# Three of the products of a fused four-layer graph kernel in float32 from one copy of their input, instead of hi and lo parts in three rounded passes

## The reference

```
L0: qkv = h @ w_qkv, 8 heads of 32; attn = softmax(where(adj == 0, -inf, q k^T * scale))
    o = (attn @ v) @ w_proj + b_proj;   x += o + layernorm(o) * gamma + beta
L1: rel = adj^T * (h Wq^T)(h Wk^T)^T, each row divided by its norm;   x += rel @ (h Wv^T)
L2: hw = h @ W (the GAT weight); e = leaky_relu(hw.a1 + (hw.a2)^T) * adj;
    x += elu(softmax(e) @ hw + beta * hw)
L3: y = adj @ h;   x += y @ weight + bias (the last weight)
```

## Time and profile before

| | |
|---|---|
| median of 3 runs | 1971.55 us (1969.12 to 1973.96) |
| profiled execution, first to last instruction | 1971.0 us (the profile gives its span; the median of the runs lies 0.5 us above it) |
| mean granted TensorE clock | 0.977 of full |
| PE busy | 1831.1 us (93%), 13064 records |
| weight loads busy | 1602.2 us (81%) |
| DVE busy | 1609.3 us (82%), 4485 |
| ACT busy | 1084.3 us (55%), 2756 |
| POOL busy | 674.6 us (34%), 1045 |
| chain that ended last | PE 48%, DVE 25%, issue 15%, POOL 9%, ACT 3% |
| ACT copy with rounding (L559, L599, L652) | 597 to 599 ns each, once a step each (L559 three times) |
| DVE lo part (L699, L778, L854) | 688, 679, 681 ns |

### The profile page before, as it was taken

How to read it: one execution, slowest core, us unless ns; L and a number is a source line. 1 busy time by engine, 2 the same in 40 slices (tenths; PEclk the granted TensorE clock), 3 DMA queues, 4 the chain that set the end, 5 groups by cost and what they waited for, 6 DMA issues and landing times.

```text
span 1971.0 us, 39957 instructions
## 1 busy us (share of the span) xinstructions
PE 1831.1 (93%) x13064; PEld 1602.2 (81%) x13064; DVE 1609.3 (82%) x4485; ACT 1084.3 (55%) x2756; POOL 674.6 (34%) x1045
## 2 busy tenths in 40 slices
PE   6899999999999999999999999999999999999974
PEld 5788888878878888888878878788888878878864
DVE  3688897888888887887888888888887988978874
ACT  3555565655655555655655655655655655655632
POOL 3233333333333333333333333333332333333331
PEclk8999999999999999999999999999999999999987
DMA  2000000000000000000000000000000000000000
GB/s 88 12 17 17 23 23 11 21 16 16 21 17 16 22 16 17 21 16 16 22 16 16 21 17 16 22 16 16 22 16 16 22 16 16 21 16 17 12 6 17
DMA packets 37975, 37.85 MB, mean 19 GB/s; under 512 B 2416, under 2 KB 37488, under 8 KB 37872
## 3 DMA queue, kind: packets, MB, share of 16 engines
q1 hardware_dynamic: 37872, 36.84, 5.7%
HBM read 20.05 MB, written 16.78 MB: 19 GB/s over the span
## 4 chain that ended last, share of the span: by engine, by line
PE 48%; DVE 25%; issue 15%; POOL 9%; ACT 3%; DVEq 0%; POOLq 0%; DMA 0%; ACTq 0%
PE bank L314 15%; PE mid L387 11%; DVE stats L683 6%; DVE x L764 5%; PE bank L322 4%; POOL o_res L909 4%; POOL rstd L899 4%; PE bank L507 3%; PE mid L370 3%; PE bank L512 3%; PE bank L487 3%; DVE x L849 3%; DVE h_t_lo L699 2%; DVE o_gam L756 2%; ACT h_t_hi L559 2%
## 5 line engine op out<-in xcount | busy, mean ns | idle before, releaser
L567 ACT ACTIVATE probs<-mid,neg_max 128x128 f32<-128x128 f32 x1024 | 284.8, 379 | 105.2 <-DVE neg_max L713 105.2
L379 PE MATMUL mid<-k_diag,q_t 128*128 128x512 f32 x512 | 273.6, 617 | 0.0
L559 ACT ACTIVATE h_t_hi<-bank 128x512 fp32r<-128x512 f32 x192 | 114.9, 599 | 251.7 <-PE bank L322 251.6
L387 PEld LDWEIGHTS mid<-v,probs_t 128*128 128x128 f32 x2048 | 244.3, 192 | 3.3
L387 PE MATMUL mid<-v,probs_t 128*128 128x33 f32 x2048 | 239.9, 272 | 0.0
L899 POOL TENSOR_TENSOR rstd<-var_eps,minus_half 128x2 f32<-128x2 f32 x320 | 226.4, 707 | 25.1
L693 DVE TENSOR_SCALAR z<-x,mean_var,rstd 128x256 f32<-128x256 f32 x384 | 205.2, 575 | 10.8 <-POOL rstd L899 3.2
L713 DVE TENSOR_REDUCE neg_max<-mid 128x8 f32<-128x1024 f32 x128 | 154.6, 1208 | 51.1 <-issue 38.0
L897 POOL TENSOR_TENSOR var_eps<-mean_var,eps 128x2 f32<-128x2 f32 x320 | 66.0, 206 | 363.9 <-DVE mean_var L687 363.9
L322 PEld LDWEIGHTS bank<-ident,z 128*128 128x128 f32 x768 | 94.8, 152 | 112.4 <-DVE z L693 73.1
L322 PE MATMUL bank<-ident,z 128*128 128x128 f32 x768 | 125.8, 288 | 61.3 <-DVE z L693 61.3
(11 more groups left out here) (133 smaller groups left out, 5485.0 us busy)
## 6 DMA issues: line engine op xcount, KB each, us to landing
x<-in_x SPq DMA_DIRECT2D x64, 256.0 KB, 2.6
out_x<-x SPq DMA_DIRECT2D x64, 256.0 KB, 2.2
w_qkv_sb<-in_w_qkv SPq DMA_DIRECT2D x1, 768.0 KB, 4.8
w_q_sb<-in_w_q SPq DMA_DIRECT2D x1, 256.0 KB, 5.0
w_k_sb<-in_w_k SPq DMA_DIRECT2D x1, 256.0 KB, 5.3
w_proj_sb<-in_w_proj SPq DMA_DIRECT2D x1, 256.0 KB, 5.2
w_v_sb<-in_w_v_t SPq DMA_DIRECT2D x1, 256.0 KB, 5.4
w_gat_sb<-in_w_gat SPq DMA_DIRECT2D x1, 256.0 KB, 5.7
```

The costliest lines, as they stand in the source:

```text
L379: last = pe.matmul(mid[:, s], q_t[:, par, hc, b * N:(b + 1) * N], k_diag[:, hc, :, b * N:(b + 1) * N], start=False, stop=True)
L387: last = pe.matmul(mid[:, b, h * W33:(h + 1) * W33], probs_t[:, b * HC + h // RG, h % RG], v0[:, par, b, h], start=True, stop=True)
L559: act.activation(h_t[k][0][:], bank[:], ACT.Relu).then_inc(h_hi_ready[k], 1)
L567: last = act.activation(probs[:, s, r], mid[:, s, r * N:(r + 1) * N], ACT.Exp, bias=neg_max[:, s, r:r + 1])
```

## The change

The lo parts of `o_t`, `h_t[2]` and `y_t` and the hi and lo parts of their weights go. ACT copies each input once, in full float32, and PE multiplies it with the float32 weight as it was loaded: `rows_f32`, four float32 matmuls (two graphs, two blocks) for each place, with the input as the stationary, as before. On DVE three operations a step go (L767, L778, L854), on POOL six of the eight operations of `split_weights`. PE waits for the one copy of ACT in place of hi and lo. The ACT copy of `o_t` gets a wait for `o_psum`, which the DVE operation had. Everything else keeps its place.

```diff
@@ -77,10 +77,7 @@
...
         w_qkv_p = parts("w_qkv", [128, C, 3 * D])
-        w_proj_p = parts("w_proj", [128, C, D])
         w_v_p = parts("w_v", [128, C, D])
-        w_gat_p = parts("w_gat", [128, C, D])
-        w_out_p = parts("w_out", [128, C, D])
         w_qk_p = parts("w_qk", [128, C, D])
@@ -115,7 +112,8 @@
...
         z = [sb(f"z{k}", [128, 2, D]) for k in range(3)]
-        h_t = [parts(f"h_t{k}", [128, C, 2 * N]) for k in range(3)]
+        h_t = [parts(f"h_t{k}", [128, C, 2 * N]) for k in range(2)]
+        h_t2_full = sb("h_t2_full", [128, C, 2 * N])
         h_t1_full = sb("h_t1_full", [128, C, 2 * N])
@@ -128,7 +126,7 @@
...
         o_heads = sb("o_heads", [128, 2, D])
-        o_t = parts("o_t", [128, 2, C, N])
+        o_t = sb("o_t", [128, 2, C, N])
         o = sb("o", [128, 2, D])
@@ -156,7 +154,7 @@
...
         h3 = sb("h3", [128, 2, D])
-        y_t = parts("y_t", [128, C, 2 * N])
+        y_t = sb("y_t", [128, C, 2 * N])
         mid = ctx.enter_context(nc.psum_tensor("mid", [128, BC, 512], f32))
...
@@ -200,9 +199,8 @@
...
             sem("u_psum"), sem("u_exp_ready"), sem("x2_exp_ready"), sem("x3_ready"), sem("x3b_ready"))
-        shift3_ready, h3_ready, y_t_psum, y_hi_ready, y_lo_ready, y_psum, x4_ready = (
-            sem("shift3_ready"), sem("h3_ready"), sem("y_t_psum"), sem("y_hi_ready"), sem("y_lo_ready"),
-            sem("y_psum"), sem("x4_ready"))
+        shift3_ready, h3_ready, y_t_psum, y_t_ready, y_psum, x4_ready = (
+            sem("shift3_ready"), sem("h3_ready"), sem("y_t_psum"), sem("y_t_ready"), sem("y_psum"), sem("x4_ready"))
         block = ctx.enter_context(nc.Block())
@@ -258,7 +256,7 @@
...
         ALL_CONSTS = 16 * len(CONSTS)
-        SPLIT = [(w_proj_sb, w_proj_p), (w_v_sb, w_v_p), (w_gat_sb, w_gat_p), (w_out_sb, w_out_p)]
+        SPLIT = [(w_v_sb, w_v_p)]
         def keys_apart(eng, p, half):
@@ -315,6 +313,14 @@
...
                 return last
+            def rows_f32(dst, lhs_t, w, signal):
+
+                for b in range(2):
+                    for c in range(C):
+                        last = pe.matmul(dst[:, b * D:(b + 1) * D], lhs_t(b, c), w[:, c], start=c == 0,
+                                         stop=c == C - 1)
+                last.then_inc(signal, 1)
+
             def transposes(dst, src, k):
@@ -405,17 +411,13 @@
...
                 if relation:
-                    pe.wait_ge(o_hi_ready, done(p3))
-                    pe.wait_ge(o_lo_ready, done(p3))
-                    for b in range(2):
-                        last = product(mid[:, 3, b * D:(b + 1) * D], o_t, w_proj_p,
-                                       lambda a, c: a[:, b, c], lambda a, c: a[:, c])
-                    last.then_inc(o_psum, 1)
+                    pe.wait_ge(o_t_ready, done(p3))
+                    rows_f32(mid[:, 3], lambda b, c: o_t[:, b, c], w_proj_sb, o_psum)
                 if front:
...
                 if middle:
-                    wait_before(pe, o_lo_ready, p2)
+                    wait_before(pe, o_t_ready, p2)
                     wait_before(pe, o_ready, p2)
@@ -442,9 +444,8 @@
...
                 if gat:
-                    pe.wait_ge(h_hi_ready[2], done(p4))
-                    pe.wait_ge(h_lo_ready[2], done(p4))
-                    rows(bank4, h_t[2], w_gat_p, 0, hw_psum)
+                    pe.wait_ge(h2_full_ready, done(p4))
+                    rows_f32(bank4, lambda b, c: h_t2_full[:, c, b * N:(b + 1) * N], w_gat_sb, hw_psum)
                 if front:
@@ -453,9 +454,8 @@
...
                 if last_layer:
-                    pe.wait_ge(y_hi_ready, done(p5))
-                    pe.wait_ge(y_lo_ready, done(p5))
-                    rows(bank7, y_t, w_out_p, 0, y_psum)
+                    pe.wait_ge(y_t_ready, done(p5))
+                    rows_f32(bank7, lambda b, c: y_t[:, c, b * N:(b + 1) * N], w_out_sb, y_psum)
                 if middle:
@@ -588,7 +588,9 @@
...
                 if gat:
-                    relu_hi(2, p4, bank4, [hw_psum])
+                    act.wait_ge(h_t_psum[2], done(p4))
+                    wait_before(act, hw_psum, p4)
+                    act.activation(h_t2_full[:], bank4[:], ACT.Relu).then_inc(h2_full_ready, 1)
                 if front:
@@ -596,7 +598,7 @@
...
                     wait_before(act, y_psum, p5)
-                    act.activation(y_t[0][:], bank7[:], ACT.Copy).then_inc(y_hi_ready, 1)
+                    act.activation(y_t[:], bank7[:], ACT.Copy).then_inc(y_t_ready, 1)
                 if middle:
@@ -649,7 +651,8 @@
...
                     act.wait_ge(o_t_psum, done(p2))
-                    act.activation(o_t[0][:], mid[:, 2], ACT.Copy).then_inc(o_hi_ready, 1)
+                    wait_before(act, o_psum, p2)
+                    act.activation(o_t[:], mid[:, 2], ACT.Copy).then_inc(o_t_ready, 1)
             run(act, step, {1: copy_fold})
@@ -763,8 +766,6 @@
...
                                                  ALU.mult, ALU.add).then_inc(x1_ready, 1)
-                if gat:
-                    relu_lo(2, p4, bank4)
                 if relation:
@@ -773,11 +774,6 @@
...
                     normalize(1, p3, z[1], x1[:, 1 - par], z_ready[1])
-                if last_layer:
-                    dve.wait_ge(y_hi_ready, done(p5))
-                    dve.tensor_tensor(y_t[1][:].rearrange("p c n -> p (c n)"), bank7[:],
-                                      y_t[0][:].rearrange("p c n -> p (c n)").bitcast(f32), ALU.subtract)\
-                       .then_inc(y_lo_ready, 1)
                 if gat:
@@ -848,12 +844,6 @@
...
                                                  x1[:, 1 - par, b], ALU.mult, ALU.add).then_inc(x2_ready, 1)
-                if middle:
-                    dve.wait_ge(o_hi_ready, done(p2))
-                    wait_before(dve, o_psum, p2)
-                    dve.tensor_tensor(o_t[1][:].rearrange("p b c n -> p (b c n)"), mid[:, 2],
-                                      o_t[0][:].rearrange("p b c n -> p (b c n)").bitcast(f32), ALU.subtract)\
-                       .then_inc(o_lo_ready, 1)
                 if gat:
```

More of the change, by code:

```diff
@@ L180, in gnn_stack @@
         h_t_psum = [sem(f"h_t_psum{k}") for k in range(3)]
-        h_hi_ready = [sem(f"h_hi_ready{k}") for k in range(3)]
-        h_lo_ready = [sem(f"h_lo_ready{k}") for k in range(3)]
+        h_hi_ready = [sem(f"h_hi_ready{k}") for k in range(2)]
+        h_lo_ready = [sem(f"h_lo_ready{k}") for k in range(2)]
+        h2_full_ready = sem("h2_full_ready")
         xb_ready, h1_full_ready = sem("xb_ready"), sem("h1_full_ready")
@@ L188, in gnn_stack @@
         heads_psum, inv_sum_ready, o_heads_ready = sem("heads_psum"), sem("inv_sum_ready"), sem("o_heads_ready")
-        o_t_psum, o_hi_ready, o_lo_ready = sem("o_t_psum"), sem("o_hi_ready"), sem("o_lo_ready")
+        o_t_psum, o_t_ready = sem("o_t_psum"), sem("o_t_ready")
         o_psum, o_ready = sem("o_psum"), sem("o_ready")
```

## The result

The changed kernel takes 1955.85 us in the median of seven runs (1949.02 to 1968.49), the kernel before 1971.79 us in seven runs (1969.12 to 1973.96). The ratio is 0.9918, with a 95% interval of 0.9896 to 0.9941: 0.8% faster, 16 us. The forecast was 1952.5 us, range 1944 to 1968. The sign, the size and the range hold. The parts of the sum don't.

The account below looks back on a forecast made before the run. Bound: the dependence loop from w_proj's product through `o`, `x1` and `z[1]` back to PE. 46 x -0.14 and 13 x -0.91 give -18.2, the ends -1: -19 from 1971.55, so 1952.5 us, range 1944 to 1968.

Parts of the forecast that it names:

- Float32's price: At each of three places on PE, eight float32 records take 1.72 us against 1.43 for the rounded passes.
- d: Extra PE time of one place in float32 over three rounded passes: about 0.30 us, bounds 0.29 and 0.45.
- the full-price rival: Float32 places on PE cost a fourth pass, d = 0.45 to 0.48: no change, 1967 to 1971 us; 16%.
- the one with bare loads: Rival: each float32 matmul of a place loses 0.08 us to stationary loads, d = 0.62: slower, 1986 us; 8%.
- w_proj in the ordinary step: PE's longer product with w_proj decides when `o` starts in an ordinary step: 0.17 us later.
- w_gat: Between `x1` and its moments, removing DVE's low part gains 0.61 us; PE's extra 0.30 hides in its wait for `z[1]`.
- `y_t_lo` costed at nothing: After `z[1]` on DVE, removing `y_t_lo` gains nothing, as DVE soon waits for ScalarE; the last weight adds 0.30 us.
- -0.14: Sum for one ordinary step in us: 0.17 - 0.61 + 0.30, counted 46 times.
- The turn: Step after a loop turn: -0.60 for `o_t_lo`, -0.61 and +0.30 give -0.91 us, 13 times.
- the turn swallows its part: Rival: DVE's 2.89 us stall ends at an unmoved time, so a turn brings only -0.31 us: 1960 us; 14%.
- More gain: POOL and DVE get out of each other's way: Rival: POOL and DVE obstruct each other less in `x1` and `z[1]` as their phase moves: about 1940 us; 2%.
- Fill and drain: First and last steps, outside the full steps: together -1 us, between -4 and +3.

Follow-up runs that it names:

- e1: The kernel before with only the w_proj place in float32, w_gat and the last weight left in rounded passes; 1941.99 us, ratio 0.9848.
- e7: The kernel before with only the w_proj place in float32, plus 12 idle instructions before DVE's loop; 1970.28 us, one run.
- e10: The changed kernel with 48 idle instructions on PE alone before the loop; 1953.91 us, ratio 0.9906.
- e9: The changed kernel with 8 idle instructions on DVE and 48 on PE before the loop; 1917.19 us, ratio 0.9723.
- e3_out_only: The kernel before with only the last weight's place in float32; 1980.88 us, ratio 1.0043.
- e12_before_pad245: The kernel before with 245 idle instructions on DVE behind step 2, before the loop; 1996.78 us, ratio 1.0120.
- e8: The kernel before with w_gat and the last weight in float32, w_proj left in three rounded passes; 1903.47 us, ratio 0.9654.
- e5: The changed kernel with 8 idle instructions on DVE before the loop; 1940.7 us, ratio 0.9854.

## Why the prediction was right, and where it was wrong

- **Float32's price.** Right. 1.72 us a place, d = 0.29 to 0.31; the full-price rival and the one with bare loads are out. The page "FP8 and Floating Point Precision" of the Trainium skill, section "TensorE Precision Notes", counts four passes; at the present price of a pass that would be 1.91 us (an estimate). The measurement decides for 1.72.
- **w_proj in the ordinary step.** Right: `o` +0.18 us (forecast +0.17), shown alone by e1 and e7 as +0.19 a step.
- **w_gat.** PE's 0.30 us was hidden in its wait for `z[1]`, as forecast. The removed low part was mis-sized: not -0.61 but -0.49. The moments must now wait until `x1` has landed: `x1` (two instructions) starts at 929.43 and the moments at 931.24, 1.81 later. Before, the low part started 1.69 after `x1` and covered that (DVE of before; the earlier trace rows has the low part at 940.88):

```profile
939.19 1.77 DVE L764 SCALAR_TENSOR_TENSOR x<-o_gam,rstd,o_res 128x256 f32<-128x256 f32 x2
```

- **`y_t_lo` costed at nothing.** This step failed. PE waited for it, 0.21 us in the ordinary step shown. The prediction saw this time, the 0.70 in place of 0.44 behind the transposes of `z[1]`, and read it as the price of a wait; with `y_t_lo` gone it is 0.49. So the last weight costs +0.02 a step and not +0.30. By parts, +0.02 at w_proj, +0.12 at w_gat and -0.28 here turn -0.14 into -0.28; the whole change has -0.255: 5 us more gain.
- **The turn.** This is the term that failed: -0.91 us forecast, -0.24 measured, 13 times: 9 us less gain. At full clock on both sides it is even +0.06; the rest is the slow clock in 8 turns before, which the prediction did not look at. The first part of the step was right; DVE's stall moved with DVE and `o` came 0.55 earlier. But I took the rest of the chain as shifted rigidly. The loop's code had moved, a second stall came with it, DVE's shift fell behind POOL's `o_res`, and the moments of `o` came 1.25 us later than they would have. The rival "the turn swallows its part" gave 1960 us by another mechanism; its number for the turn, -0.31, was nearer than the forecast's. Its reason is refuted: the 2.9 us moved with DVE's arrival, and `o` came earlier.
- **"More gain: POOL and DVE get out of each other's way"** was named with 2%. That their phase can get worse by 1.25 us a turn was not.
- **Fill and drain:** -4.3 against -1, just beyond the bound of -4. Not taken apart.

So the time is right by luck in part: errors of +5, -9 and +3 us nearly cancel. And the 16 us say little of the change's worth: with the same work, the changed kernel ran at 1953.9, 1940.7 and 1917.2 us, depending on idle instructions ahead of its loop. In long turns on both sides the change is worth about 18 us (1972 to 1954), or 21 to 22 without the 3 to 4 us that e10's idle instructions cost. Some 12 of them are the ordinary steps and 7 the slow clock that its turns no longer have; the shift's loss of 1.25 us a turn is already taken off. A comparison in short turns on both sides was not reached. Of the 55 us between before and e9, 0.255 x 59 = 15 come from the steps' work; most of the rest is the turn: 32.29 us before, 29.01 in e9.

What stays open: why the clock falls in some turns of the kernel before and not in others; a test of the condition on the loop's place that is given at the end; why PE's stalls come in some turns only; and the 3 us of fill and drain.

## What to carry to other kernels

Price each place of a change by itself, and look at each of them in the timeline: here one part of three brought all the gain in the ordinary steps, one cost 0.19 us a step, and the best kernel leaves that part out. A wait on several semaphores hides its second operand; an "issue" of 0.24 us on a weight load was a DVE operation that I took as free. In a kernel with a loop, look at the stall at each turn first, in every version that is compared: its length can change with any edit on that engine. The profile's instruction packets and 8 or 12 idle instructions tell whether a difference is the work or the place of the loop. Where steps that do the same work differ in length, look at the granted clock in each before anything else.

## What the runs showed of the hardware

- A turn back costs DVE 0.35 or about 3 us, by where the loop lies in its instruction stream: 0.35 at 449-827, 450-820 and 453-831; 2.9 to 3.3 at 442-812, 456-838, 457-839, 460-846, 461-839, 465-843 and 474-844, and long too at 705-1091. A long turn comes with five instruction packets of 8 KB on q14, a short one with none. PE had stalls of 3.3 to 5 us at irregular turns with its loop starting at 2198, each with nine packets of 16 KB on q8, and never over 0.3 us with starts of 2243 and more.
- The Trainium skill, page "Runtime: NRT & Kernel Launch", section "Instruction fetch mechanics", says that instructions come in blocks of 256 (16 KiB), that most engines hold two blocks and PE eight, that the next is fetched while the current one runs, and that a branch to a block no longer held stalls. The trace agrees in kind: the stalls come with instruction packets. It does not agree that two blocks are enough: with a block starting at 449, 456-838 would lie in two and be short, but it was long. DVE's packets are of 8 KB, which by the Trainium skill's figure would be 128 instructions (an estimate). With it, one reading fits all fourteen kernels: no reload when the loop lies in three packets of 128 on DVE (449 to 833) and in seven of 256 on PE (2241 to 4033), each edge up to two earlier. The short DVE positions lie in 449 to 833, all long ones begin before it or end beyond it; 705-1091 ends beyond 1089, the edge of the three packets from 705. The quiet PE loops, counted in the built programs, lie between 2243 and 4024. The kernel before, with 386 instructions on DVE, would then fit nowhere. The reading was made after the runs, and none was made to test it.
- The granted clock fell to half for 3.4 us in 8 of 13 turns of the kernel before, 12 of e3_out_only and all 13 of e12_before_pad245, and in none of e7, e8, e9 and e10. In the kernel before such a turn took 32.61 us in place of 31.77.
- A small DVE operation on 128x2 elements took 0.15 us, and 0.78 to 1.09 us when POOL's 128x512 addition had begun before it: it ended 0.01 to 0.02 us after POOL's, in 12 turns of the changed kernel and 13 of e10. The moments of `o`, beside the same addition, weren't held up.
- A float32 matmul of 256 columns costs 0.43 us in a stream and three rounded ones 0.36, so float32 is only a fifth dearer here, for one operand copy instead of two.
- An idle wait instruction on DVE costs 0.096 us when nothing hides it (23.5 us for 245); 48 on PE lengthened step 3 by 4.1 us in e10 and by 2.7 in e9 (against the changed kernel and e5).
